# A fused scan kernel: B by transposes of copied rows, and a third of the scaling by B in four of sixteen states on GpSimd

## What is computed

```
h = tok(x)                                   # softmax(q k^T / 16) v, q = k = v = x, per segment
h = h + scan_block(layernorm(h))
h = h + moe(layernorm(h))                    # 64 experts, the 8 best of 4 groups, 256 slots each

scan_block(x):  x_in, z = split(x @ W_in.T)  # 512 channels each
  u  = silu(conv4(x_in) + b_conv)
  dt = softplus(u @ W_dt.T + b_dt)
  B, C = u @ W_B.T, u @ W_C.T                # 16 states each
  for each token:  h = exp(dt*A) * h + (dt*u) * B;   y = sum over states of h * C
  return (y * silu(z)) @ W_out.T
```

## Time and profile before

| | |
|---|---|
| Median of 3 runs | 3737.77 us (3730.68 to 3738.78) |
| The profiled execution | 3755.1 us, span 3752.9 us |
| Mean granted TensorE clock | 0.95 of full speed |
| Busy: TensorE, VectorE, ScalarE, GpSimd | 3115.0, 2904.9, 2874.3, 2106.4 us |
| The 16 states of sequence 14 | 1452.5 to 1549.4 us from the span's start |

### The profile page before, as it was taken

One profiled execution on the slowest core, in us unless ns is written; L12 is line 12 of the kernel. 1 busy time (PEld: TensorE's weight loads), 2 busy tenths in 40 slices (PEclk: granted clock), 3 DMA queues, 4 the chain that ended last, 5 costly groups with the idle time before them and its releaser, 6 DMA issues. The chain is left out here.

```text
span 3752.9 us, 63833 instructions
## 1 busy us (share of the span) xinstructions
PE 3115.0 (83%) x19681; PEld 2513.8 (67%) x19681; DVE 2904.9 (77%) x4755; ACT 2874.3 (77%) x5580; POOL 2106.4 (56%) x780
## 2 busy tenths in 40 slices
PE   5889888888888888888888888888888887566664
PEld 3777777677777777777777777677677777544543
DVE  2777888888888888888888888888888888544442
ACT  4989899888889888988898889888888888121110
POOL 0655555555555555555555555555555557157776
PEclk9999999999999999999999999999999999678897
DMA  2111111111111111111111111111111111167775
GB/s 85 40 40 54 58 57 58 58 49 58 57 36 57 58 58 58 58 58 54 53 58 58 58 54 45 58 58 58 50 58 45 49 52 51 43 139 150 148 151 87
DMA packets 175718, 241.44 MB, mean 64 GB/s; under 512 B 32816, under 2 KB 154128, under 8 KB 175376
## 3 DMA queue, kind: packets, MB, share of 16 engines
q1 hardware_dynamic: 150800, 199.44, 16.6%
q0 software_dynamic: 24576, 37.77, 6.1%
HBM read 176.07 MB, written 61.08 MB: 63 GB/s over the span
## 5 line engine op out<-in xcount | busy, mean ns | idle before, releaser
L349 POOL TENSOR_TENSOR hid<-hid,c_all 128x1536 f32<-128x1536 f32 x512 | 1771.1, 3459 | 1437.4 <-DVEq L561 1434.2
L566 DVE TENSOR_TENSOR_SCAN hid<-decay,hid,psB 128x1024 f32<-128x1024 f32 x512 | 1201.6, 2347 | 171.5 <-PE psB L830 131.2
L367 ACT ACTIVATE dbu_t<-dtu_t,b_t 128x512 f32<-128x512 f32 x1536 | 995.0, 712 | 275.9 <-PE psB L830 275.4
L830 PE MATMUL psB<-ident,dbu_t 128*128 128x128 f32 x6144 | 884.5, 281 | 309.0 <-DVE hid L566 295.7
L379 ACT ACTIVATE decay<-dt,a_neg 128x383 f32<-128x383 f32 x2048 | 1086.4, 606 | 0.0
L830 PEld LDWEIGHTS psB<-ident,dbu_t 128*128 128x128 f32 x6144 | 701.4, 144 | 463.6 <-DVE hid L566 389.2
L842 PE MATMUL psY<-ident,hid 128*128 128x128 f32 x6144 | 788.3, 280 | 3.5 <-POOL hid L349 3.5
L566 DVE TENSOR_TENSOR_SCAN hid<-decay,psB 128x512 f32<-128x512 f32 x512 | 624.1, 1219 | 186.9 <-PE psB L830 161.6
L842 PEld LDWEIGHTS psY<-ident,hid 128*128 128x128 f32 x6144 | 718.6, 146 | 3.7 <-POOL hid L349 3.7
L902 PE MATMUL psM<-u,w_dt 128*128 128x384 f32 x1024 | 352.0, 487 | 3.8 <-ACT soft L413 2.0
L902 PEld LDWEIGHTS psM<-u,w_dt 128*128 128x128 f32 x1024 | 184.6, 190 | 106.9 <-ACT soft L413 3.2
(11 more groups left out here) (148 smaller groups left out, 3544.9 us busy)
## 6 DMA issues: line engine op xcount, KB each, us to landing
c_all<-bc_rows_dram SPq DMA_DIRECT2D x128, 768.0 KB, 4.8
out_dram<-h SPq DMA_DIRECT2D x64, 384.0 KB, 4.0
h<-out_dram SPq DMA_DIRECT2D x32, 384.0 KB, 3.4
x_weights_dram<-normed SPq DMA_DIRECT2D x32, 384.0 KB, 2.4
xs<-in_x_dram SPq DMA_DIRECT2D x32, 256.0 KB
e_wg<-in_gate_dram SPq DMA_DIRECT2D x64, 128.0 KB
e_wu<-in_up_dram SPq DMA_DIRECT2D x64, 128.0 KB
e_wd<-in_down_dram SPq DMA_DIRECT2D x64, 128.0 KB
```

The costliest lines, as they stand in the source:

```text
L349: nc.gpsimd.tensor_tensor(hid[k % 4][:, :, :], hid[k % 4][:, :, :], c_all[:, k, :].unsqueeze(1).to_broadcast([P, CH, L]), ALU.mult).then_i ...
L367: last = nc.scalar.activation(dbu_t[k % 2][:, t, :], dtu_t[q][:, t, :], ACT.Copy, scale=b_t[q][:, t, k:k + 1])
L566: nc.vector.tensor_tensor_scan(h[:, lo:hi], flat(decay[k % 4])[:, lo:hi], flat(psB)[:, lo:hi], h[:, lo - 1:lo] if j else 0.0, ALU.mult, AL ...
L830: last = nc.tensor.transpose(flat(psB)[:, i * P:(i + 1) * P], dbu_t[k % 2][:, t, c * P:(c + 1) * P], ident[:, :])
```

## The change

Three edits, all in `sequence_phase`. (1) The matmuls of L913 are gone. Instead the rows of B and C, copied to SBUF for the DMA anyway, are turned in state 14 by three 128x128 transposes into a product BT of its own, between YT2 and O1 in the second slot; for that `bc_rows` has 128 partitions, of which 96 are zeroed once. ScalarE copies B out of it at the start of state 14. (2) On ScalarE the second half of the softplus moves behind the copy of the turned probabilities. (3) In the states 3, 8, 12 and 13 ScalarE scales two of the three token blocks, and GpSimd the third, in its queue right after the product with C three states earlier. TensorE waits for both.

```diff
+POOL_PART = (3, 8, 12, 13)
-           ("XN1", ..., "S", "PT", "CB", "AT1", "YT1", "DU1", "YT2", "O1", "LG"))
+           ("XN1", ..., "S", "PT", "CB", "AT1", "YT1", "DU1", "YT2", "BT", "O1", "LG"))
-        bc_rows = sb("bc_rows", [2 * NS, L])
+        bc_rows = sb("bc_rows", [P, L])
@@ GpSimd
+            def scaled_part(b, q, k):
+                s = NS * b + k
+                pool.wait_ge(s_bs, s)
+                pool.wait_ge(s_bt, PB * (s - 1))
+                t = NSEG - 1
+                nc.gpsimd.tensor_tensor(dbu_t[k % 2][:, t, :], dtu_t[q][:, t, :],
+                                        b_t[q][:, t, k:k + 1].to_broadcast([P, DI]), ALU.mult).then_inc(s_bp, 1)
-            with pool.Fori(0, NB) as b:
-                for k in range(NS):
-                    times_c(b, k)
+            with pool.Fori(0, NB // 2) as i:
+                for q in range(2):
+                    for k in range(NS):
+                        times_c(2 * i + q, k)
+                        if k + 3 in POOL_PART:
+                            scaled_part(2 * i + q, q, k + 3)
@@ ScalarE
-                for t in range(NSEG):
+                for t in range(NSEG - (k in POOL_PART)):
...
-                nc.scalar.activation(b_t[r][:, :, :].rearrange("p t n -> p (t n)"),
-                                     psM[slot("CB")][:, L:L + NSEG * NS], ACT.Copy)
-                nc.scalar.activation(bc_rows[:, :], psM[slot("CB")][0:2 * NS, 0:L],
+                nc.scalar.activation(bc_rows[0:2 * NS, :], psM[slot("CB")][0:2 * NS, 0:L],
                                      ACT.Copy).then_inc(s_out[slot("CB")], 1)
+            def copy_b(b, r):
+                filled("BT", b)
+                nc.scalar.activation(b_t[r][:, :, :], psM[slot("BT")][:, 0:L].rearrange(
+                    "p (t n) -> p t n", t=NSEG)[:, :, 0:NS], ACT.Copy).then_inc(s_out[slot("BT")], 1)
...
+                    if front and k == 14:
+                        copy_b(b, r)
                     if of:
                         scaled_dbu(*of)
...
-                        if k == 8:
-                            softplus(n, b, 1)
...
                     if early and k == 8:
                         copy_prob_t(b)
+                    if front and k == 8:
+                        softplus(n, b, 1)
@@ TensorE, turn_dbu
                     pe.wait_ge(s_bs, s + 1)
+                    if k in POOL_PART:
+                        pe.wait_ge(s_bp, len(POOL_PART) * b + POOL_PART.index(k) + 1)
@@ TensorE, project_bc
-                for t in range(NSEG):
-                    for k in range(CH):
-                        last = nc.tensor.matmul(to[:, L + t * NS:L + (t + 1) * NS], u[:, k, t * P:(t + 1) * P],
-                                                w_bc[:, k, 0:NS], start=(k == 0), stop=(k == CH - 1))
+            def turn_b(b):
+                copied("CB", b)
+                emptied("BT", b)
                 for t in range(NSEG):
+                    last = nc.tensor.transpose(psM[slot("BT")][:, t * P:(t + 1) * P],
+                                               bc_rows[:, t * P:(t + 1) * P], ident[:, :])
+                last.then_inc(s_in[slot("BT")], 1)
...
+                        if k == 14:
+                            turn_b(b)
                     if back:
```

More of the change, by code:

```diff
@@ L52 @@
 LATE = ("X2T0", "X2T1", "LG")
+POOL_PART = (3, 8, 12, 13)
 SLOTTED = (("XN0", "X0", "X2", "Z0", "Z2", "D0", "D1", "D2", "X2T0", "D3", "X2T1", "AT0", "YT0", "DU0", "DU2", "O0"),
-           ("XN1", "X1", "X3", "Z1", "QT0", "QT1", "S", "PT", "CB", "AT1", "YT1", "DU1", "YT2", "O1", "LG"))
+           ("XN1", "X1", "X3", "Z1", "QT0", "QT1", "S", "PT", "CB", "AT1", "YT1", "DU1", "YT2", "BT", "O1", "LG"))
 def sequence_phase(nc, x, w, bc_dram, h_out, x_tab, ch_tab):
@@ L163, in sequence_phase @@
         s_bs = sem("dbu_scaled")
+        s_bp = sem("dbu_last_part_scaled")
         s_bt = sem("dbu_turned")
@@ L275, in store_bc @@
                 wait(s_out[slot("CB")], number("CB", b))
-                sp.dma_start(bc_dram[r], bc_rows[:, :]).then_inc(s_bcw, 16)
+                sp.dma_start(bc_dram[r], bc_rows[0:2 * NS, :]).then_inc(s_bcw, 16)
                 wait(s_bcw, 16 * (n + 1))
@@ L363, in scaled_dbu @@
                     act.wait_ge(s_out[slot("DU2")], number("DU2", b - 1))
-                    act.wait_ge(s_out[slot("CB")], number("CB", b - 1))
+                    act.wait_ge(s_out[slot("BT")], number("BT", b - 1))
                 after(act, s_bt, PB * (s - 1))
-                for t in range(NSEG):
+                for t in range(NSEG - (k in POOL_PART)):
                     last = nc.scalar.activation(dbu_t[k % 2][:, t, :], dtu_t[q][:, t, :], ACT.Copy,
@@ L548, in _ @@
             nc.vector.memset(xin[:, :, 0:TAPS - 1], 0.0)
+            nc.vector.memset(bc_rows[:, :], 0.0)
             nc.vector.memset(epsc[:, :], EPS)
@@ L909, in project_bc @@
                 for k in range(CH):
-                    nc.tensor.matmul(to[0:2 * NS, 0:L], w_bc[:, k, :], u[:, k, :], start=(k == 0), stop=(k == CH - 1))
+                    last = nc.tensor.matmul(to[0:2 * NS, 0:L], w_bc[:, k, :], u[:, k, :], start=(k == 0),
+                                            stop=(k == CH - 1))
+                last.then_inc(s_in[slot("CB")], 1)
+            def turn_b(b):
+                copied("CB", b)
+                emptied("BT", b)
                 for t in range(NSEG):
-                    for k in range(CH):
-                        last = nc.tensor.matmul(to[:, L + t * NS:L + (t + 1) * NS], u[:, k, t * P:(t + 1) * P],
-                                                w_bc[:, k, 0:NS], start=(k == 0), stop=(k == CH - 1))
-                last.then_inc(s_in[slot("CB")], 1)
+                    last = nc.tensor.transpose(psM[slot("BT")][:, t * P:(t + 1) * P],
+                                               bc_rows[:, t * P:(t + 1) * P], ident[:, :])
+                last.then_inc(s_in[slot("BT")], 1)
             def turn_dtu(n, b, t):
```

## The result

The changed kernel takes 3614.8 us (median of 4 runs, 3613.8 to 3615.6) against 3738.3 us before: a ratio of 0.967 [0.965, 0.969]. The forecast was 3614.

A forecast was written before the change was run, and what follows sets the result against it. No engine is full; TensorE's work in state 9, then VectorE, sets the pace. 30 x (2.70 + 0.94 - 0.33) = 99.3 us, plus 4.7 at the ends and 20 from the clock, make 124: 3614 us, range 3596 to 3660.

The forecast's parts named there:

- L913 goes, -2.70 us: State 9, TensorE: removing 24 small matmuls before the turn VectorE awaits saves 2.70 us per sequence.
- The softplus moves, -0.94 us: State 9: ScalarE copies the turned probabilities earlier, so TensorE's 0.94 us wait before the B and C rows goes.
- Rival (b): State 10: VectorE's L664 or the decays take over and the 0.94 us do not come through: 3642 us; chance 0.10.
- The next four states carry it on: States 10 to 14: VectorE carries 3.64 us forward; without GpSimd's help ScalarE would be some 0.6 us late, costed at nothing.
- Three transposes, +0.33 us: State 14, TensorE: three transposes of B right before the output projection add 0.33 us to the path.
- GpSimd's part, 1.2 us, worth 0: States 3, 8, 12, 13: one 128x512 multiplication on GpSimd takes 1.2 us and changes the path by 0 us.
- Rival (d): Behind states 1, 6, 10, 11: VectorE and GpSimd hold each other up, convolution included, giving 3764 us; chance 0.05.
- a sign of being wrong: The forecast is wrong if VectorE's instructions behind states 1, 6, 10 and 11 get longer; no size given.
- The clock, 20 us: State 10 to 11: TensorE's granted clock no longer falls once L913 and the wait go, saving 20 us in all.
- Rival (c): TensorE: transposes lower the clock, a fall in each of 31 sequences and no 20 us back: 3686 us; chance 0.04.
- The sum: Whole kernel: 124 us saved together, 3614 us against the median and 3631 against the profiled execution.

The follow-up runs named there:

- without the offload: The changed kernel with an empty list of GpSimd states, so ScalarE scales all three thirds in every state: 3616.6 us.
- the run beside it: The changed kernel with GpSimd's third taken in states 4 and 5 instead of 3 and 8, beside VectorE's convolution: 3664.4 us.
- B alone: The kernel before with only B turned by three transposes in state 14 instead of L913's matmuls; softplus and scaling as before: 3653.4 us.
- softplus alone: The kernel before with only the second half of the softplus moved behind the copy of the turned probabilities: 3703.4 us.
- offload alone: The kernel before with only GpSimd's thirds of the scaling in states 3, 8, 12 and 13: 3740.4 us, ratio 1.001.
- offload in thirteen states: The changed kernel with GpSimd's third taken in all thirteen states from 3 to 15: 3681.9 us.

## Why the prediction was right

- **L913 goes, -2.70 us.** Right: 2.73 alone, and nothing took its place. VectorE's wait of 4.25 us became 0.57 (0.6 forecast).
- **The softplus moves, -0.94 us.** Right: 1.01 alone. Rival (b), that VectorE's L664 or the decays would take over, did not happen: they ended at 1450.11 and 1449.91, the scan started at 1450.68.
- **The next four states carry it on.** Right: 10 to 14 kept their distances to 0.03 us. The 0.6 us by which ScalarE was to be late without the offload was too much. Without it the same distances stand, and the wait of 1.14 us that ScalarE has with it before the scaling of state 14 is just used up. With the offload first, then without it, where the scaling follows the decays at once:

```profile
1463.10 1.95 ACT L382 ACTIVATE dbu_t<-dtu_t,b_t 128x512 f32<-128x512 f32 x3 [1.14 <-PE psB L853]
...
1473.18 0.20 ACT L446 ACTIVATE b_t<-psM 128x48 f32<-128x48 f32 x1
1473.55 1.95 ACT L382 ACTIVATE dbu_t<-dtu_t,b_t 128x512 f32<-128x512 f32 x3 [0.17 <-ACT b_t L446]
```

```profile
1459.82 2.11 ACT L394 ACTIVATE decay<-dt,a_neg 128x383 f32<-128x383 f32 x4
1461.86 1.95 ACT L382 ACTIVATE dbu_t<-dtu_t,b_t 128x512 f32<-128x512 f32 x3
```

In both the scaling starts 0.40 us before the first scan of state 12 (1463.50 and 1462.26), so without the offload ScalarE is not late at all there.

- **Three transposes, +0.33 us.** Right: 0.32. A copy of B (L446) and a wait of 0.17 us before the scaling stand in the first block above, hidden by the 2.56 us for which ScalarE waits next.
- **GpSimd's part, 1.2 us, worth 0.** Both right; it takes 1.04 us, and no TensorE wait for it beyond one of 0.8 us shows in the execution. The product and the part behind it, and what VectorE does meanwhile, as the earlier trace rows:

```profile
1398.45 3.45 POOL L352 TENSOR_TENSOR hid<-hid,c_all 128x1536 f32<-128x1536 f32 x1 [4.42 <-DVEq L582]
1401.85 1.04 POOL L362 TENSOR_TENSOR dbu_t<-dtu_t,b_t 128x512 f32<-128x512 f32 x1
```

```profile
1401.97 1.86 DVE L597 TENSOR_TENSOR yz_t<-psY,zs_t 128x512 f32<-128x512 f32 x3
1403.75 1.14 DVE L677 SCALAR_TENSOR_TENSOR u<-xin,w_cv,u 128x384 f32<-128x384 f32 x2
```

The gate takes 1.86 us as before. Rival (d) named the convolution as the place; the run beside it showed the mechanism and its price (up to 0.87 us a part, against the 1.2 assumed), and that the states of the change miss it. Of the other VectorE work named there the row maximum, the statistics and the scans kept their durations. But one instruction behind state 6 did get longer, which the prediction had named as a sign of being wrong: L605, which multiplies the three row maxima by a constant and reads one SBUF tile. VectorE, then GpSimd:

```profile
1432.33 0.53 DVE L602 TENSOR_REDUCE rmax<-psM 128x3 f32<-128x384 f32 x1
1432.90 0.43 DVE L605 TENSOR_SCALAR nmax<-rmax 128x3 f32<-128x3 f32 x1
```

```profile
1432.25 1.06 POOL L362 TENSOR_TENSOR dbu_t<-dtu_t,b_t 128x512 f32<-128x512 f32 x1
```

It takes 0.41 to 0.51 us in the 27 sequences in which a part runs beside it, where it takes 0.17 in the kernel before and without the offload, and it ends within 0.03 us of the part's end (27 x 0.26 = 7 us of busy time). So a VectorE instruction with a single SBUF input was held too. It cost nothing: without the offload VectorE is idle for 0.24 us before the scan behind it, and state 6 to 7 takes 4.57 us either way. That this place had room was not in the prediction, so the 0 there is luck in part.
- **The clock, 20 us.** The amount was right at its place (21.7 us in state 10 to 11, no fall left), and B alone shows no fall there without L913; with L913 in place but not the wait before it (softplus alone) 4 were left. But the rows did not show where others would come. 7.8 us were won at state 0, and new falls in states 11 and 12 cost some 3.5 us in 14 to 15 (13.4 less 31 x 0.32). Rival (c), transposes that lower the clock, is not borne out, though it named a place where the clock does fall. In the pure transposes of states 11 and 12, which showed 1.00 in the window of the earlier trace rows, falls rose from 2 to 14, and to 29 with the transposes in state 11. Yet they rose to 10 in softplus alone too, with no transpose added, and were only 4 in B alone and 7 with the transposes in state 12 (15 there without the offload). What they cost is plain: without a fall state 14 to 15 takes 5.60 to 5.62 us in the steady sequences of the changed kernel, and 6.10 to 6.19 with one. What sets them stays open.
- **The sum.** Per sequence 3.31 us were forecast and 3.67 - 0.32 - 0.09 = 3.26 measured. Against the profiled execution the forecast was 3631 and the profile says 3614.5, 16.5 us less: 5 more in state 9, mostly in the first three sequences (4.3 to 5.8 us each), 8 at state 0, 5 more before the first and behind the last scan, and small terms of both signs. That the median was met to 1 us is luck in part: the terms fell 16.5 us short of what the profiled executions differ by, and that of before happened to lie 17 us above its median.
- **Not foreseen:** 0.09 us more from state 8 to 9. It comes with the change of B (also in B alone and without offload, not in softplus alone or offload alone). Its cause stays open.

## What to carry to other kernels

Price an edit at the place where the wait ends last: 2.70 us of small matmuls in front of the one turn that VectorE awaited were worth 90 us (some 20 of them where the clock no longer fell), some 80 us of relief on a busy but waiting engine nothing. Before an operation is put into a gap, look at who holds its buffer and not only at the gap, and then count where the clock falls; one state decided between 8 us won and 25 lost. Work for GpSimd held up VectorE's instructions with two SBUF inputs, however short, until it was through, and here also a three-element multiplication by a constant with one SBUF input. Beside the scans, the gate and the statistics it was free.

## What the runs showed that was not expected

The granted clock is part of the schedule. With the same instructions, moving three transposes by one state changed the falls of states 11 and 12 from 7 to 29 of 58 (6 and 18 of 29 sequences), and each such sequence took 0.5 to 1.4 us more from state 14 to 15 (none more in the offload in thirteen states). The falls behind state 0 have a place of their own: in all the kernels they stand in even sequences alone, behind the end of an odd one, where the code's loop over two sequences goes round and state 15 to the next state 0 takes 6.8 to 7.2 us instead of 6.0 (6.4 to 6.8 instead of 5.6 in the offload in thirteen states). An edit that repeats six transposes cost 20 us by its own length and another 11 at a place half a sequence away. Moving a softplus, with L913 left in place, took the falls behind state 10 from 14 to 4 (the offload alone, which changes no time, had 11). For a change of under 10 us on such a kernel the falls have to be counted in the trace before the difference is put down to the edit.
